# Clipping the values of chunks 1 to 3 on GpSimd instead of VectorE, in a quantized vision transformer layer

## What is computed

```python
def fake_quant(q, s, z):
    zr = ste_round(z)
    return s * (jnp.clip(ste_round(q / s) + zr, 0.0, QMAX) - zr)
...
qkv = fake_quant(x, sx1, zx1) @ fake_quant(ww1, sw1, zw1).T
q, k, v = jnp.split(qkv, 3, axis=-1)
...
dots = jnp.einsum('bhnd,bhmd->bhnm', fake_quant(q, sq, zq), fake_quant(k, sk, zk)) * scale
a = jax.nn.softmax(dots, axis=-1)
out = jnp.einsum('bhnm,bhmd->bhnd', fake_quant(a, sa, za), fake_quant(v, sv, zv))
...
return fake_quant(out, sx2, zx2) @ fake_quant(ww2, sw2, zw2).T + bb2
```

## Time and profile before

| what | value |
|---|---|
| median of 3 runs | 173.92 us (172.39 to 173.94) |
| the profiled execution's own time | 171.95 us |
| its span, first to last instruction | 170.2 us |
| mean granted TensorE clock, share of full | 0.907 |
| PE busy | 137.1 us, 81% |
| DVE busy | 130.0 us, 76% |
| ACT busy | 118.8 us, 70% |
| POOL busy | 44.4 us, 26% |

### The profile page before, as it was taken

How to read it: one execution, slowest core, us unless ns; L and a number is a source line. 1 busy time by engine, 2 the same in 40 slices (tenths; PEclk the granted TensorE clock), 3 DMA queues, 4 the chain that set the end, 5 groups by cost and what they waited for, 6 DMA issues and landing times.

```text
span 170.2 us, 5210 instructions
## 1 busy us (share of the span) xinstructions
PE 137.1 (81%) x1846; PEld 109.4 (64%) x1846; DVE 130.0 (76%) x391; ACT 118.8 (70%) x232; POOL 44.4 (26%) x108
## 2 busy tenths in 40 slices
PE   0499789998688969779977987715899999999960
PEld 0499577955455545546565765611389999999940
DVE  2626965999999999995999978669977676766750
ACT  8934457579899989998998746710277787777610
POOL 7212533341000022010112017864002222422242
PEclk9999999999999999995996557655799999999999
DMA  3799999999999999500000002342792100010000
GB/s 78 289 308 294 309 393 222 222 221 320 367 370 364 370 369 385 231 4 0 4 0 4 2 6 95 120 170 109 190 382 86 46 15 27 27 35 27 4 27 24
DMA packets 12922, 27.72 MB, mean 163 GB/s; under 512 B 1745, under 2 KB 8667, under 8 KB 12897
## 3 DMA queue, kind: packets, MB, share of 16 engines
q1 hardware_dynamic: 11744, 24.41, 45.5%
q0 software_dynamic: 1152, 2.97, 4.8%
HBM read 15.39 MB, written 12.29 MB: 163 GB/s over the span
## 4 chain that ended last, share of the span: by engine, by line
PE 38%; DVE 18%; issue 14%; ACT 13%; DMA 8%; SPq 4%; POOL 2%; POOLq 0%; ACTq 0%; DVEq 0%
PE lin_bank L1358 12%; DMA patches<-in_patches 8%; PE head_bank L1097 4%; PE head_bank L1370 3%; PE head_bank L1378 3%; PE head_bank L1371 3%; PE lin_bank L1391 3%; ACT vint L504 2%; ACT w L522 2%; PE lin_bank L1130 2%; ACT ex L528 2%; DVE row L890 2%; SPq L326 2%; PE lin_bank L1126 2%; DVE dif L760 2%
## 5 line engine op out<-in xcount | busy, mean ns | idle before, releaser
L643 ACT ACTIVATE q<-lin_bank,b 128x128 f32<-128x128 f32 x72 | 25.0, 369 | 7.4 <-PE lin_bank L1358 6.7
L1358 PE MATMUL lin_bank<-q,w 128*128 128x128 f16 x360 | 29.6, 219 | 0.5 <-ACT q L633 0.5
L1358 PEld LDWEIGHTS lin_bank<-q,w 128*128 x360 | 23.7, 98 | 0.9 <-issue 0.8
L1097 PE MATMUL head_bank<-proj_w,patches 128*128 128x192 f32 x84 | 17.8, 372 | 7.1 <-DMA patches<-in_patches 7.1
L1097 PEld LDWEIGHTS head_bank<-proj_w,patches 128*128 128x128 f32 x84 | 16.4, 222 | 7.4 <-issue 6.6
L430 POOL TENSOR_TENSOR rstd<-veps,nhalf 128x1 f32<-128x1 f32 x7 | 4.7, 667 | 55.7 <-DVE veps L700 55.7
L1370 PE MATMUL head_bank<-early,q 128*128 x72 | 17.7, 246 | 0.3 <-DVE q L1073 0.3
L1068 DVE CAST q<-q 128x384 f16<-128x384 f32 x24 | 8.6, 360 | 12.0 <-ACT q L643 12.0
L1378 PE MATMUL head_bank<-early,q 128*128 x72 | 17.7, 246 | 0.0
L1371 PE MATMUL head_bank<-early,q 128*128 x72 | 17.7, 246 | 0.0
L1130 PE MATMUL lin_bank<-xqT,ww1q 96*128 96x288 bf16 x96 | 15.4, 286 | 2.4 <-ACT kint L510 1.2
(11 more groups left out here) (158 smaller groups left out, 352.6 us busy)
## 6 DMA issues: line engine op xcount, KB each, us to landing
slots<-blank SPq DMA_DIRECT2D x3, 2938.0 KB, 22.3
patches<-in_patches SPq DMA_DIRECT2D x9, 384.0 KB, 11.8
early<-in_ww SPq DMA_DIRECT2D x3, 576.0 KB, 11.0
patches<-in_w SPq DMA_DIRECT2D x4, 384.0 KB, 11.6
patches<-in_w SPq DMA_DIRECT2D x8, 192.0 KB, 13.2
patches<-in_w SPq DMA_DIRECT2D x2, 576.0 KB, 12.9
v<-slots SPq DMA_DIRECT2D x5, 226.0 KB, 3.8
patches<-slots SPq DMA_DIRECT2D x4, 226.0 KB, 4.7
```

Of the source, the lines that this page charges most:

```text
L643: a.activation(g[:, j % 2, m], up_bank[n % 4][:, 0:P], ACT.Gelu, scale=1.0 / WSCALE, bias=b1[:, bass.ds(e, 1), m]).then_inc(g_ok, 1)
L1097: last = mm(emb_bank[t][:, 0:E], patches[:, t, kc], proj_w[:, kc], start=kc == 0, stop=kc == KE - 1)
L1358: last = mm(up_bank[n % 4][:, 0:P], up_weights(j, part, m), xT[:, j % 3, piece], start=x == 0, stop=x == len(PASSES) - 1)
```

## The change

GpSimd clips the values of pairs 4 to 15 (chunks 1 to 3), twelve instructions of 128x768 from 16-bit integers to bf16; VectorE keeps those of pairs 0 to 3. GpSimd clips a pair in the step in which ScalarE rounds it, the first of two ahead of that step's `scale`, the second behind it. `norm_low(t)` stands now at step 7 + 2t ahead of both, and `scale(t)` at step 5 + 2t. A new semaphore `pool_v_ok` counts GpSimd's clips: ScalarE waits for it before it reuses a `vint` buffer, and TensorE before `attend` of pairs 4 to 15.

```diff
--- before.py
+++ after.py
@@ -236,7 +236,7 @@
         aT_ps, aT_ok, o_ps, o_int, o_ok = map(sem, ("aT_ps", "aT_ok", "o_ps", "o_int", "o_ok"))
         pr_ps, h2_ok, xn_ok, xhi_ok, xlo_ok, xnT_ps, xnT_ok, gate_ps = map(sem, (
             "pr_ps", "h2_ok", "xn_ok", "xhi_ok", "xlo_ok", "xnT_ps", "xnT_ok", "gate_ps"))
-        pool_lo_ok = sem("pool_lo_ok")
+        pool_lo_ok, pool_v_ok = map(sem, ("pool_lo_ok", "pool_v_ok"))
         whi_ok, wlo_ok, route, onehot_ok, count_ps, logit_ok, slot_ok, slot_row_ok, expert_ok = map(sem, (
             "whi_ok", "wlo_ok", "route", "onehot_ok", "count_ps", "logit_ok", "slot_ok", "slot_row_ok", "expert_ok"))
         slotT_ps, slotT_ok, up_ps, g_ok, ghi_ok, glo_ok, down_ps, res_ok, y_ok = map(sem, (
@@ -449,10 +449,29 @@
                 gp.tensor_tensor(row16[:, t, LO:LO + E], xn[:, t % 2], row16[:, t, HI:HI + E],
                                  ALU.subtract).then_inc(pool_lo_ok, 1)
 
-            for t in range(6):
-                scale(t)
-                if 1 <= t <= POOL_LOWS:
-                    norm_low(t - 1)
+            def clip_values(p):
+                pool.wait_ge(lin_int, lin_no[("v", p // PPC, p % PPC)] + 1)
+                if p >= VB:
+                    pool.wait_ge(o_ps, p - VB + 1)
+                gp.tensor_scalar(v[:, p % VB], vint[:, p % 2], lo[:, VQ:VQ + 1], hi[:, VQ:VQ + 1],
+                                 ALU.max, ALU.min).then_inc(pool_v_ok, 1)
+
+            def values_of(i):
+
+                return [c * PPC + n for kind, c, n in lin_groups(i) if kind == "v" and c]
+
+            pool.wait_ge(scales_ok, 1)
+            for i in range(STEPS):
+                for t in tiles_at(i, 3):
+                    if t < POOL_LOWS:
+                        norm_low(t)
+                for p in values_of(i)[:1]:
+                    clip_values(p)
+                for t in tiles_at(i, 1):
+                    scale(t)
+                for p in values_of(i)[1:]:
+                    clip_values(p)
+            scale(5)
             scatter(0, 0, 1)
             scale(6)
             scatter(0, 1, 2)
@@ -500,7 +519,10 @@
                     if p == 0:
                         act.wait_ge(w_quant, 6)
                     if p >= 2:
-                        act.wait_ge(v_ok, p - 1)
+                        if p - 2 < PPC:
+                            act.wait_ge(v_ok, p - 1)
+                        else:
+                            act.wait_ge(pool_v_ok, p - 1 - PPC)
                     a.activation(vint[:, p % 2].rearrange("p (s n) -> p s n", s=2), bank[:, :, 0:INNER // 2],
                                  ACT.Copy, scale=rv).then_inc(lin_int, 1)
                     return
@@ -732,10 +754,7 @@
                         dve.wait_ge(s_ps, (c - 1) * PPC)
                     clip(k[:, c % 2], kint[:], KQ).then_inc(k_ok, 1)
                 else:
-                    p = c * PPC + n
-                    if p >= VB:
-                        dve.wait_ge(o_ps, p - VB + 1)
-                    clip(v[:, p % VB], vint[:, p % 2], VQ).then_inc(v_ok, 1)
+                    clip(v[:, n], vint[:, n % 2], VQ).then_inc(v_ok, 1)
 
             def clips_of(i):
 
@@ -931,7 +950,7 @@
                         weights(n)
                 for t in tiles_at(i, 1):
                     project(t)
-                clipped = clips_of(i - 1) if i else []
+                clipped = [x for x in clips_of(i - 1) if x[0] != "v" or x[1] == 0] if i else []
                 values = [x for x in clipped if x[0] == "v"]
                 if old:
                     inverse(p)
@@ -1172,7 +1191,10 @@
 
             def attend(p):
                 pe.wait_ge(aT_ok, p + 1)
-                pe.wait_ge(v_ok, p + 1)
+                if p < PPC:
+                    pe.wait_ge(v_ok, p + 1)
+                else:
+                    pe.wait_ge(pool_v_ok, p + 1 - PPC)
                 if p == 0:
                     pe.wait_ge(h_ok, TT)
                 if p >= 1:
```

## The result

The change makes the kernel slower: 183.93 us median of four runs (182.91 to 185.65) against 173.56 for the kernel before in the same series, a ratio of 1.062 with an interval of 1.052 to 1.072. That is 10.4 us, outside the stated range, whose upper end was 178.2. The profiled execution took 182.91 us with a span of 181.1, against 171.95 and 170.2 before.

What follows compares the result with a forecast made beforehand. The loop over pairs was taken to run at ScalarE's pace, VectorE just behind. Steps 3 and 4 +0.56, 7 and 8 0, 11 and 12 +0.28 gave +0.84, taken as +0.9: 173.92 + 0.9 = 174.8 us, range 172.6 to 178.2.

Steps and rivals of the forecast that it cites:

- The GpSimd clip: Each of the twelve clips added on GpSimd was taken as 1.25 us, from a conversion of 128 elements.
- upper bound of 1.9 us: Bound from above on one GpSimd clip, from a two-input subtraction with 16-bit output at 2.35 ns an element.
- rival 1: Short GpSimd clip of 0.74 us blocks VectorE 0.54; gains stay inside ScalarE's waits, 173.4 us; chance 0.20.
- The root behind the clip: In GpSimd's queue, roots of tiles 1 and 3 come 0.4 us late each, counted as adding nothing to the blocking.
- rival 4: Roots queued behind a GpSimd clip add their 0.4 + 0.4 us to the forecast: 175.6 us; chance 0.08.
- the prediction's own sign: Mechanism wrong if VectorE's records keep their lengths, or VectorE or ScalarE waits over 0.5 us for GpSimd in a step.
- The port: On the shared port, a pair's second GpSimd clip stops VectorE for 1.25 - 0.2 = 1.05 us; the first is mostly hidden.
- its length less 0.2: Rule that a GpSimd operation costs a contending VectorE instruction its own length less 0.2 us, from the token clip at 39.27.
- the forecast's +0.28 us a pair: Net cost to VectorE of a pair: 1.05 us blocked against 0.77 us freed.
- ScalarE's wait for a buffer: ScalarE's copy waits for the clip two copies earlier; taken as nothing, with 0.9 us of slack at the tightest.
- The removal: Twelve clips leaving VectorE free 4.6 us, of which at best 1.1 counts, from ScalarE's waits behind steps 3 and 4.
- Rival 3: Long GpSimd clip, deciding from about 1.45 us: both of a pair block VectorE; 177.0 at 1.6 us, 180.0 at 1.9; chance 0.22.

Runs made afterwards that it cites:

- p1: The kernel before plus single GpSimd operations behind its last output, alone and beside VectorE operations; a two-limit clip of 768 took 2.92 us alone.
- e1: The changed kernel with the roots (and norm_low) of a step ahead of both value clips in GpSimd's loop; 176.97 us, ratio 1.028 to the kernel before.
- e4: The kernel before, VectorE's clips kept, plus five tiny GpSimd powers at each place of the changed kernel's clips, in its queue order; 179.71 us, ratio 1.044.
- e3: The kernel before, VectorE's clips kept, plus twelve GpSimd clips of constant data with unused results, roots first; 177.78 us, ratio 1.031.
- e9: e8 plus twelve GpSimd clips of constant data at the places of e6, results unused; 175.99 us, ratio 1.019 to the kernel before.
- e8: The kernel before without the twelve value clips of chunks 1 to 3 on any engine; 173.18 us, ratio 1.005.
- e5: e1 with three vint buffers in place of two; 175.56 us, ratio 1.025 to the kernel before.
- e6: e5 with some clips issued later, so that no root stands behind a clip of the step before; 176.1 us, ratio 1.019 to the kernel before.
- e2: The changed kernel's idea for chunk 1 only: GpSimd clips pairs 4 to 7, VectorE the rest; 173.94 us, ratio 1.006 to the kernel before.
- e7: e2 with three vint buffers; 174.67 us, ratio 1.009 to the kernel before.

## Why the prediction was wrong

**The GpSimd clip, taken as 1.25 us.** This is the step that failed first, and it took the sizes of the waits below with it. It is 2.92 us alone (p1) and 2.99 in the kernel, and even the upper bound of 1.9 us, from the slope of a two-input subtraction, lay under it. The row I held to be the nearest, the conversion of 128 elements, was the wrong kin: I took its 289 ns less 96 as a slope of 1.5 ns, but the conversion of 768 (from 16-bit integers, the short one from f32) takes 0.82 us, so it has a slope of (822 - 289) / 640 = 0.83 ns and a larger fixed part. And each limit adds to it, as p1 shows. One short row gave me a slope that it did not have, of a kind of work that lacks the limits. The Trainium skill (GPSIMD Engine Reference, Elementwise — side-by-side cycle accounting) would have given less still: rival 1's estimate of 0.66 us is under a quarter of the measured time.

**The root behind the clip, put at nothing in the forecast, or 0.4 + 0.4 us in rival 4.** The mechanism was seen and is the largest term: 3.19 and 4.41 us of waiting, about 6 us of time by e1 and 7.7 by e4. It was sized with the short clip, and with a queue that is empty when the pair arrives. With 2.93 us the pair of the step before is still running, so that two clips and a low half stand ahead of the root, not one. I also judged it to be "the same wait" as the port's; e4 shows that it is one by itself, without any blocked instruction. By the prediction's own sign, a wait for GpSimd of more than 0.5 us in a step, the mechanism had failed here, and not the size alone.

**The port, taken as 1.05 us a pair for a clip of 1.25.** e3 gives 0.39 us a clip, 0.79 a pair, for a clip of 2.9 us. The rule "its length less 0.2" fits the 0.59 us operation and not a long one. With the measured 2.99 us in it my sum for the port would have been 2.79 + 1.59 - 0.77 = 3.6 us a pair, 7.2 + 4.9 + 6.9 = 19 us in all and a time of 193: as far off on the other side, and by a blocking that e3 did not find. The rule, not only the clip's length in it, was wrong. That the forecast's +0.28 us a pair lies near what was measured (0.79 given back against 0.77 freed) is luck, two wrong sizes that met. That this costs time although VectorE's sum hardly changes was not in the forecast: e9 against e8 is 2.5 us. The likely reason, argued and not shown, is that the freed time falls where VectorE then waits for ScalarE, as in e8, while the blocking falls on the product and the clip of probabilities, for which TensorE waits.

**ScalarE's wait for a buffer, taken as nothing with 0.9 us of slack.** The wait is 2.6 us in the changed kernel and 3.0 in e1; what it costs in time, 0.5 to 1.4 us by e5, is not resolved. A failure of the clip's length again.

**The removal, at most 1.1 us of 4.6.** The reading of the idle times was right in that VectorE does not set the pace: e8 gives no measurable gain. The 1.1 us of steps 3 and 4 was read wrongly: ScalarE's two waits there are 0.78 and 0.33 us in e8 as well, because VectorE spends what it saves waiting for ScalarE's half of the weights (L522) at the splits of steps 3 and 4, before the difference on which those waits hang.

**Rival 3, the long clip,** had the right side and the right condition, and 180.0 us as its extreme; it got 0.22, and the range was cut in its middle. But it priced the long clip by the port alone, which is not where most of the time went. By the runs, in per cent of the kernel before: roots 3.4 (the changed kernel to e1), buffers 0.3 (to e5), later clips 0.6 (to e6), what is left 1.9. These add up to 6.2 by construction, since each kernel contains the edits of the last; independent of them are e4 for the roots, 4.4, and e9 for what is left, 1.9, of which 1.4 is the port's by e8 and the other 0.5 no more than the noise.

## What to carry to other kernels

An engine with spare time is not a free helper: ask first what short instructions it has in its queue that others wait for, and put them ahead of the long new ones, since the queue's order cost here 3.4 per cent and the shared port 1.4. Never size an unseen operation from one short row of another kind; measure it in two sizes, as a slope and a fixed part, and let the range reach to where the forecast breaks. And an engine busy for over 90% of a stage need not be its bound if it waits now and then for one at 100%: remove its work entirely once, as e8 did, before looking for a place to move it to.

## What the runs showed of the hardware that was not expected

A GpSimd clip stops VectorE in parts of its length only, and which VectorE instruction is stopped seems to depend on the part. From VectorE's timeline of the changed kernel beside the clip at 67.03 to 69.96 and one at 89.68 to 92.6:

```profile
68.80 0.50 DVE L892 SCALAR_TENSOR_TENSOR aint<-ex,inv,rden 108x288 int16<-108x288 f32 x1
69.34 0.70 DVE L704 TENSOR_SCALAR aq<-aint,lo,hi 108x288 bf16<-108x288 int16 x1
...
91.66 0.51 DVE L892 SCALAR_TENSOR_TENSOR aint<-ex,inv,rden 108x288 int16<-108x288 f32 x1
```

The product ran at its usual 0.51 us from 1.8 to 2.3 us after the clip's start, and again from 2.0 to 2.5 us in the other; the clip of probabilities, begun 2.3 us after the start, ended at 70.04, just behind the GpSimd clip. Early in a clip both kinds were stopped: the normalization at 77.60, 0.04 us behind the start of a clip, took 1.05 us in place of 0.37, and the product at 48.92, 0.54 us behind the start of the first clip, 0.75 in place of 0.51. It looks as if the clip reads in its first third and writes in its last; that is a reading of a few rows, and no run tried it by itself. Nor is it the whole rule: in e1 the clip of probabilities at 73.60, 0.05 us behind the start of a GpSimd clip and close behind another contending instruction of VectorE, kept its 0.34.

TensorE's clock differs between executions that are alike so far. The granted clock from 46 to 48 us, by stretch (last three columns clock, DMA share, GB/s), for the kernel before, for p1 and for e4:

```profile
46.00:48.00 2.00, 1.79 (x40) 0.92 (x38) 2.00 (x5) 2.00 (x4) 0.00 (x0) 1.00 1.05 370
```

```profile
46.00:48.00 2.00, 2.00 (x40) 1.25 (x40) 2.00 (x7) 1.89 (x4) 0.00 (x0) 0.79 1.05 371
```

```profile
46.00:48.00 2.00, 1.77 (x40) 0.92 (x37) 2.00 (x5) 2.00 (x4) 1.19 (x3) 1.00 1.05 370
```

p1 is the kernel before up to its last output, and yet was at half clock (1.2 GHz) for part of this time, as were the changed kernel, e1, e2, e3, e7, e8 and e9; before, e4, e5 and e6 were at full clock (2.4 GHz). So the dip is not the change's doing. What makes the clock fall is not seen here. It delays ScalarE's copy at 46 us by up to 0.9 us (its wait is 1.68 us in e9 and 1.56 in e8, 0.76 in the profile of before), and the step behind it gets longer: from the difference at 47.74 us to the next it is 3.88 us before, 5.03 at the same place in p1 and 5.19 in e8, two kernels with no GpSimd clip there. That is nearly all of the 1.4 us by which e8's profile is longer than that of before. The changed kernel has 5.65 there, so 1.2 to 1.3 of the 10.9 us between the two profiled spans are likely the clock's. Single profiles of these kernels are therefore not to be compared to better than one or two microseconds, and repeated runs are used above.
